# When the rows of one batch are scattered: as a burst at the start of the next batch, or spread over its first cross attention

## The chip, the cores and the metric

The kernel runs on one NeuronCore of a Trainium2 chip, as one launch. The metric is the device time of a run in microseconds. A core has five engines with queues of their own: TensorE (PE: matmuls and transposes), VectorE (DVE), ScalarE (ACT), GpSimd (POOL) and SyncE (SP, which here issues most of the DMAs). They wait for one another only through semaphores.

## The reference

A decoder of two layers on `x` of 4 batches x 512 tokens x 256 features, each sublayer behind a layer norm and with a residual:

```python
x = x + _L0_attn_ref(_layernorm(x), ...)    # A: 16 heads of 64, scores refined by a small MLP over heads
x = x + _L0_xattn_ref(_layernorm(x), ctx_1024, ctx_1024, ...)  # B: 16 heads of 16, 1024 keys
x = x + _L0_ffn_ref(_layernorm(x), ...)     # C: switch-head attention
x = x + _L1_attn_ref(_layernorm(x), ...)    # D: causal, rope
x = x + _L1_xattn_ref(_layernorm(x), ctx_1024, ctx_1024, mask, ...)  # E: masked cross attention
x = x + _L1_ffn_ref(_layernorm(x), ...)     # F and G: a mixture of 32 experts, 8 of them for each token
```

In the last line each token's normalized row goes through the 8 experts that a gate picks, weighted, and through two shared experts.

## The kernel before

**Rounds and stages.** The four batches are four rounds. A round has six stages, A to F, one for each line above (F: the gate and the shared experts). Each of the five engines has its own program, written in the same order of stages: a hardware loop over the rounds (`Fori`) with the six stages in its body. SP runs its loop three times and has the fourth round written out. After each stage all five meet at a barrier (`Steps.end`: a drain, a semaphore increment, a wait for all five), and `end_round` is the last of these in a round. After the four rounds stage G does the chosen experts for all batches at once.

**Scattering.** Stage F computes, for each token, the 8 places in a DRAM tensor `slot_rows` (one region per expert) where its row must go (`slot8`), and completes the row in SBUF, `xn`: 256 normalized features, the token's number, 32 expert weights, 290 float32 in all. `to_slots` (L1356) then scatters `xn` to `slot_rows` in 32 indirect DMAs issued by POOL: 4 tiles of 128 tokens x 8 places, 128 rows of 1160 B each (L1360). In POOL's program it stands behind `end_round` (L2223 and on), so its 32 DMAs are issued while the other engines are in stage A of the next round, or, for the last batch, in the start of stage G. Each adds 16 to the semaphore `scattered`, which only SP waits for, late in stage G.

**`xn` and the layer norms.** `ln_dve` (L389) does the layer norm between two stages: statistics, one power on POOL (`ln_pool`, L406), then four scaled tiles into `xn`; `ln_pe` (L430) transposes `xn` for the next stage. Stage A doesn't write `xn` itself (its input comes from `f_xnA`, made in stage F of the round before), but the layer norm between A and B does.

**The head of stage A.** PE projects q and k (L1757), multiplies them to scores (L1781) head by head and projects values (L1768) in between; DVE turns q and k by rope (L1956 to L1962); ACT copies each block of scores out of PSUM into `a_fin` (L1916); SP stores them to DRAM in another layout (L1710) and loads them back. The head ends when PE starts the small MLP (L1798). PE's next scores wait for ACT's copy (`s_up`), ACT waits for PE's scores (`s_mm`), DVE for the projections (`qk_mm`).

**Stage B.** After projections and 12 x 6 moves of q and k parts to their places (L455, issued by SP), an inner loop runs over 16 heads in pairs: PE scores (L532) for DVE's row maxima (L771), turned scores (L588) for ACT's exponentials (L709, 128 of them, semaphore `exp`), then the weighted sum (L605). DVE splits each head's maxima in three bfloat16 parts by small operations (L739 to L742). `OT`, a buffer of attn16_mem in SBUF, takes the finished heads' sums (L717); nothing uses it before the inner loop.

Of the kernel before, what the change touches and what calls it, by code (L numbers as in the profile page):

```python
# [22 lines left out]
P = 128  # L23
B, S, DM = 4, 512, 256
NI = S // P
# [5 lines left out]
STAGES = "ABCDEF"  # L31
# [161 lines left out]
TOPK = 8  # L193
# [26 lines left out]
def y_tile(ps, stage, i):  # L220

    if stage == "C":
        return ps[:, 2 + i, 0:Y_COLS]
    return ps[:, 7 - i // 2, (i % 2) * Y_COLS:(i % 2 + 1) * Y_COLS]
# [5 lines left out]
def decoder(nc, io, out, rounds=B):  # L230
    ctx = ExitStack()
    with ctx:
        def sb(name, shape, dt=F32):
            return ctx.enter_context(nc.sbuf_tensor(name, shape, dt))

        def sem(name):
            s = ctx.enter_context(nc.semaphore(name))
            counting.append(s)
            return s
# [4 lines left out]
        x = sb("x", [P, NI, DM])  # L244
        xn = sb("xn", [P, NI, ROW])
        xnT = sb("xnT", [P, KD, S])
        ctxT = sb("ctxT", [P, KD, CTX])
        ident = sb("ident", [P, P])
# [27 lines left out]
        slot8 = sb("slot8", [P, NI, TOPK], U32)  # L276
# [15 lines left out]
        ps = ctx.enter_context(nc.psum_tensor("ps", [P, 8, BANK], F32))  # L292
# [10 lines left out]
        scattered = ctx.enter_context(nc.semaphore("scattered"))  # L303
# [3 lines left out]
        ln_pow = sem("ln_pow")  # L307
        ln_xn = sem("ln_xn")
# [11 lines left out]
        sm = {}  # L320
# [8 lines left out]
        def scope(fn):  # L329
            with ExitStack() as inner:  # L330
                return fn(lambda name, shape, dt=F32: inner.enter_context(nc.sbuf_tensor(name, shape, dt)))
# [22 lines left out]
            return m  # L354

        M16 = scope(attn16_mem)

        WIDTH = {"B": 2560, "D": 3584, "E": 2560, "C": 3616}
        ORDER = [s for s in "BCDE" if s in STAGES]
# [6 lines left out]
        def ln_stats(ch, rows, var, early=()):  # L366
            for i in set(range(NI)) - set(early):
                last = nc.vector.bn_stats(out=st6[:, i, :], in_=rows(i))
            ch.link(last)
            for i in range(NI):  # L370
                last = nc.vector.bn_aggr(out=mv[:, i, :], in_=st6[:, i, :])
            ch.link(last)
            nc.vector.tensor_scalar(mv[:, :, 1], mv[:, :, 1], 1e-5, None, ALU.add).then_inc(var, 1)  # L373

        def ln_scaled(dve, ch, rows, powered, n, done, to=xn):
            dve.wait_ge(powered, n + 1)

            ch.link(nc.vector.tensor_tensor(rt[:, :], rstd[:, :], rstd[:, :], ALU.mult))
            ch.link(nc.vector.scalar_tensor_tensor(out=rt[:, :], in0=rt[:, :], scalar=-0.5, in1=mv[:, :, 1], op0=ALU.mult, op1=ALU.mult))
            ch.link(nc.vector.scalar_tensor_tensor(out=rstd[:, :], in0=rt[:, :], scalar=1.5, in1=rstd[:, :], op0=ALU.add, op1=ALU.mult))  # L380
            for i in range(NI):
                nc.vector.tensor_scalar(to[:, i, 0:DM], rows(i), mv[:, i, 0:1], rstd[:, i:i + 1],
                                        ALU.subtract, ALU.mult).then_inc(done, 1)
# [5 lines left out]
        def ln_dve(dve, ch, n, before):  # L389
            if before == "A":  # L390
                ln_stats(ch, lambda i: x[:, i, :], ln_var, EARLY[before])
                ln_scaled(dve, ch, lambda i: x[:, i, :], ln_pow, n, ln_xn)
                return
            rows = lambda i: y_tile(ps, before, i)
            ln_stats(ch, rows, ln_var, EARLY[before])
            ln_scaled(dve, ch, rows, ln_pow, n, ln_xn)
            if before == "C":
                last = nc.vector.tensor_copy(x[:, :, :], ps[:, 2:2 + NI, 0:Y_COLS])
            else:
                for h in range(2):  # L400
                    last = nc.vector.tensor_copy(x[:, 2 * h:2 * h + 2, :], ps[:, 7 - h, :].rearrange("p (i c) -> p i c", i=2))
            last.then_inc(x_kept, 1)

        def ln_pool(pool, n):
            pool.wait_ge(ln_var, n + 1)
            nc.gpsimd.tensor_tensor(rstd[:, :], mv[:, :, 1], half[:, :], ALU.pow).then_inc(ln_pow, 1)  # L406
# [21 lines left out]
                nc.tensor.matmul(ps[:, bank, :], identb[:, :], mneg[:, 0, 0:BANK], start=True, stop=True)  # L428

        def ln_pe(pe, n):  # L430
            for i in range(NI):
                pe.wait_ge(ln_xn, NI * n + i + 1)
                for k in range(KD):
                    last = nc.tensor.transpose(ps[:, k, i * P:(i + 1) * P], xn[:, i, k * P:(k + 1) * P], ident[:, :])
            last.then_inc(ln_tr, 1)

        def ln_act(act, n):
# [6 lines left out]
        def a16_sp(sp, c):  # L444
            m = M16
            g = lambda n: sm[c.name, n]
            sp.dma_start(m["KS"][KR:KST, :, :].rearrange("p h n -> p (h n)").bitcast(mybir.dt.uint16), io["k_unit"].partition_broadcast(3)).then_inc(g("k_ones"), 16)
            for kind, t, gr in c.moves:
                n = S if kind == "q" else c.nk
                stack, parts, order = (m["QS"], m["QP"], QPART) if kind == "q" else (m["KS"], m["KP"], KPART)  # L450
                last = max(k for k, e in enumerate(c.split_order) if c.tiles[e][:2] == (kind, t))
                sp.wait_ge(g("split"), last + 1)
                first, width = HEAD_GROUPS[gr]
                for r, a in enumerate(order):
                    sp.dma_start(stack[HD * r:HD * (r + 1), 8 * t + first:8 * t + first + width, 0:n],  # L455
                                 parts[HD * first:HD * (first + width), a, t, 0:n]).then_inc(g(f"stack_in{3 * t + gr}"), 16)

        def a16_pool(pool, ch, c):
            vp = M16["VP"][:, 0:c.nj, :, :].rearrange("p j h d -> p (j h) d")
            ch.link(nc.gpsimd.memset(vp[:, :, HD:32], 0.0))  # L460
            nc.gpsimd.memset(vp[:, :, HD:HD + 1], 1.0).then_inc(sm[c.name, "v_zero"], 1)

        def a16_pe(pe, c, n):
            m = M16
            g = lambda s: sm[c.name, s]
# [193 lines left out]
        def a16_act(act, c, n):  # L659
            m = M16  # L660
            g = lambda s: sm[c.name, s]
# [70 lines left out]
        def a16_dve(dve, ch, c):  # L732
            m = M16
            g = lambda s: sm[c.name, s]
# [159 lines left out]
        C_BACK = {s + 1: q for s, q in C_WEIGH.items()}  # L894

        def c_pe(pe, _, n, st):
            m = MC
            g = lambda s: sm["C", s]
# [289 lines left out]
        slot_rows = nc.dram_tensor("slot_rows", (NE * ROOM + P, ROW), F32, kind="Internal").ap()  # L1188
# [164 lines left out]
        EXTRA["F"] = dict(pe=f_pe, act=f_act, dve=f_dve, pool=lambda pool, *_: next_pool(pool), sp=f_sp)  # L1353


        def to_slots(pool):  # L1356

            for i in range(NI):
                for k in range(TOPK):
                    nc.gpsimd.indirect_dma_start(out=slot_rows, out_offset=bass.IndirectOffsetOnAxis(ap=slot8[:, i, k:k + 1], axis=0),  # L1360
                                                 in_=xn[:, i, :], in_offset=None).then_inc(scattered, 16)

        RX, RT, RH, RY = 9, 3, 3, 24
        NT = B * NI
# [73 lines left out]

        def g_pool(pool):
            g = lambda s: sm["G", s]  # L1440
            pool.wait_ge(x_stored, 16)
            pool.wait_ge(zeroed, 16 * NACC)
            for b in range(NBLOCK):
                pool.wait_ge(g("y_up"), b + 1)
                if b >= NACC:
                    pool.wait_ge(g(f"added{b % NACC}"), 16 * (b // NACC))
                nc.gpsimd.indirect_dma_start(out=sums[b % NACC], out_offset=bass.IndirectOffsetOnAxis(ap=token[:, b % RY:b % RY + 1], axis=0),  # L1447
                                             in_=MG["y"][:, b % RY, :], in_offset=None, compute_op=ALU.add).then_inc(g(f"added{b % NACC}"), 16)
# [767 lines left out]
        @block.gpsimd  # L2216
        def _(pool):
            st = Steps(pool, bars, False)
            setup_pool(pool)
            st.end()  # L2220
            st.end_round()
            with pool.Fori(0, rounds) as b:
                ch = Chain(pool, pool_chain)  # L2223
                for n, s in enumerate(STAGES):
                    if n:
                        ln_pool(pool, n - 1)
                    if s in CFG:
                        a16_pool(pool, ch, CFG[s])
                    else:
                        EXTRA[s]["pool"](pool, ch, n, st)  # L2230
                    st.end()
                st.end_round()
                to_slots(pool)
            g_pool(pool)

        @block.scalar
# [172 lines left out]
```

## Time and profile before

| | |
|---|---|
| median of 3 runs | 3875.18 us (3869.48 to 3879.73) |
| the profiled execution's own time | 3884.64 us |
| its span, first to last instruction | 3882.9 us |
| PE busy | 3455.5 us (89%) |
| DVE busy | 2416.0 us (62%) |
| ACT busy | 1803.9 us (46%) |
| POOL busy | 512.9 us (13%) |
| POOL, the 128 scattering DMAs, L1360 | 127.5 us, 996 ns each |

How to read it: the span holds a short setup, four rounds of some 850 to 875 us, and stage G of some 380 us. A busy share is a mean over stages; what a change in one stage is worth is read in that stage. The time of an indirect DMA on POOL is that of its issue, not of its transfer.

### The profile page before, as it was taken

The numbers are of one execution on the slowest core, as the hardware profiler recorded it, in microseconds if no ns is written. First come the engines' busy times: TensorE is split into PE (matmuls) and PEld (weight loads), VectorE is DVE, ScalarE is ACT, GpSimd is POOL, SyncE is SP. The second block draws the span as 40 slices with busy tenths as digits, with TensorE's granted clock in tenths as the row PEclk, the third lists the DMA queues.
The fourth block names the chain that finished last, engine by engine and source line by source line (L and its number), as shares of the span: only waits on it lengthen the run. The fifth ranks groups of instructions, "written<-read, shape, count | busy, mean of one in ns | idle before, by whom it ended". The sixth has DMA issues, their size and how long they took to land.

```text
span 3882.9 us, 62857 instructions
## 1 busy us (share of the span) xinstructions
PE 3455.5 (89%) x21953; PEld 1668.0 (43%) x21953; DVE 2416.0 (62%) x6385; ACT 1803.9 (46%) x3597; POOL 512.9 (13%) x451
## 2 busy tenths in 40 slices
PE   6999989997999889996999889997999889997992
PEld 2352445343362445342352445343352445344772
DVE  5668576854668576853668576853668576853553
ACT  2755434442755434442755434442745434442441
POOL 0000020003000020003000020003000020006885
PEclk9999999998999999998999999998999999997996
DMA  6313001215313001214313001215313201847998
GB/s 211 115 39 64 20 6 48 46 58 157 109 40 63 20 8 46 46 58 150 115 39 64 20 7 47 45 58 167 107 35 61 90 9 46 234 160 172 160 161 172
DMA packets 184288, 317.59 MB, mean 82 GB/s; under 512 B 29972, under 2 KB 139412, under 8 KB 178580
## 3 DMA queue, kind: packets, MB, share of 16 engines
q1 hardware_dynamic: 152888, 270.90, 25.1%
q0 software_dynamic: 29040, 39.86, 5.8%
q8 instruction: 187, 3.06, 0.3%
q10 hardware_dynamic: 2032, 2.61, 0.2%
q14 instruction: 141, 1.16, 0.1%
HBM read 176.94 MB, written 116.70 MB: 76 GB/s over the span
## 4 chain that ended last, share of the span: by engine, by line
PE 68%; DVE 19%; ACT 4%; issue 3%; another core or an unknown queue 3%; DMA 1%; PEldq 1%; SPq 1%; POOL 0%; DVEq 0%; PEld 0%; POOLq 0%; ACTq 0%
PE ps L605 8%; PE ps L588 6%; PE ps L428 5%; PE ps L532 4%; DVE mx L771 4%; PE ps L1860 4%; PE ps L1467 3%; PE ps L593 3%; PE ps L1798 3%; PE ps L484 2%; PE ps L1781 2%; DVE ps L768 2%; PE ps L1757 2%; PE ps L1482 2%
## 5 line engine op out<-in xcount | busy, mean ns | idle before, releaser
L709 ACT ACTIVATE PT<-ps 128x512 f32<-128x512 f32 (+2 forms) x1280 | 643.8, 564 | 332.8 <-PE ps L593 174.6
L771 DVE TENSOR_REDUCE mx<-ps 128x1 f32<-128x512 f32 (+3 forms) x768 | 431.0, 617 | 91.6 <-PE ps L532 49.1
L588 PE MATMUL ps<-QS,KS 99*128 99x512 bf16 (+2 forms) x1280 | 421.1, 370 | 8.5 <-ACT PT L709 8.0
L532 PE MATMUL ps<-KS,QS 96*128 96x512 bf16 (+3 forms) x1280 | 397.1, 373 | 17.5 <-DVE mx L771 7.3
L406 POOL TENSOR_TENSOR rstd<-mv,half 128x4 f32<-128x4 f32 x20 | 20.3, 1016 | 2829.8 <-DVE mv L373 2829.8
L768 DVE CUSTOM_DVE_ANT_0 ps<-ps,mneg 128x512 f32<-128x512 f32 x512 | 340.7, 718 | 82.2 <-PE ps L532 79.0
L605 PE MATMUL ps<-PT,VP 128*32 128x512 f32 (+3 forms) x2560 | 377.1, 577 | 0.0
L428 PE MATMUL ps<-mneg,identb 128*128 128x512 bf16 x1240 | 330.6, 395 | 29.3 <-DVE a_fin L1975 10.9
L588 PEld LDWEIGHTS ps<-QS,KS 99*128 99x128 bf16 x1280 | 108.6, 97 | 395.5 <-ACT PT L709 234.5
L1447 POOL DMA_INDIRECT sums<-wbuf,ctxT x159 | 247.9, 1559 | 57.4 <-issue 37.2
L1975 DVE TENSOR_TENSOR a_fin<-a_fin,ps 128x512 f32<-128x512 f32 (+1 forms) x176 | 104.5, 635 | 210.2 <-PE ps L1840 208.7
L532 PEld LDWEIGHTS ps<-KS,QS 96*128 96x128 bf16 x1280 | 128.4, 100 | 226.0 <-DVE mx L771 74.2
L698 ACT ACTIVATE QS<-ps 3x512 bf16<-3x512 f32 x192 | 113.3, 590 | 234.1 <-PE ps L570 231.7
L1940 ACT ACTIVATE a_X<-ps,b1A 128x1024 f32<-128x1024 f32 (+2 forms) x152 | 169.3, 1157 | 73.4 <-PE ps L1804 72.8
L593 PE MATMUL ps<-mnegT,identb 128*128 128x512 bf16 x512 | 194.6, 380 | 0.0
L428 PEld LDWEIGHTS ps<-mneg,identb 128*128 128x128 bf16 x1240 | 119.0, 101 | 167.1 <-issue 32.0
L1916 ACT ACTIVATE a_fin<-ps 128x2048 f32<-128x2048 f32 (+1 forms) x64 | 79.2, 1237 | 214.8 <-PE ps L1781 116.4
L1467 PE MATMUL ps<-g_W,g_xT 128*128 x636 | 167.3, 386 | 4.9 <-issue 4.9
L1757 PE MATMUL ps<-wbuf,a_Y 128*128 128x512 f32 x256 | 134.0, 668 | 22.3 <-issue 12.1
L791 DVE RECIPROCAL rq<-ps 128x16 f32<-128x16 f32 x48 | 12.4, 258 | 224.7 <-PE ps L542 224.7
L1928 ACT ACTIVATE a_fin<-a_fin,a_nm 128x512 f32<-128x512 f32 (+3 forms) x256 | 140.5, 550 | 2.2 <-DVE a_nm L1985 1.6
L1360 POOL DMA_INDIRECT slot_rows<-xn,slot x128 | 127.5, 996 | 78.1 <-remote 40.3
(332 smaller groups left out, 6020.7 us busy)
## 6 DMA issues: line engine op xcount, KB each, us to landing
slot_rows<-in_padrows SPq DMA_DIRECT2D x32, 725.0 KB, 19.8
scores<-a_fin SPq DMA_DIRECT2D x64, 256.0 KB
a_fin<-scores SPq DMA_DIRECT2D x32, 512.0 KB, 4.6
KS<-KP SPq DMA_DIRECT2D x240, 64.0 KB, 2.6
g_xb<-slot_rows SPq DMA_DIRECT2D x105, 145.0 KB
a_Y<-in_wA SPq DMA_DIRECT2D x4, 3072.0 KB, 13.6
scores<-a_fin SPq DMA_DIRECT2D x64, 192.0 KB
a_fin<-scores SPq DMA_DIRECT2D x12, 1024.0 KB, 7.9
```

The lines of the kernel that those rows point to most:

```text
L428: nc.tensor.matmul(ps[:, bank, :], identb[:, :], mneg[:, 0, 0:BANK], start=True, stop=True)
L532: last = nc.tensor.matmul(o, m["QS"][0:KR, h, i * P:(i + 1) * P], m["KS"][0:KR, h, f:f + w], start=True, stop=not c.causal)
L588: last = nc.tensor.matmul(o, m["KS"][0:KST, h, j * P:(j + 1) * P], m["QS"][0:KST, h, q0:S], start=True, stop=plain)
L593: last = nc.tensor.matmul(o, identb[:, :], mnegT[:, j, :], start=False, stop=True)
L605: last = nc.tensor.matmul(ps[r:r + 32, 6, q0:S], m["VP"][:, j, h, :], m["PT"][:, mp % 2, j % 2, e, 0:S - q0], start=(j == 0), stop=(j == c ...
L709: nc.scalar.activation(m["PT"][:, mp % 2, j % 2, e, 0:w], ps[:, SLOTS + n % TURNED, 0:w], ACT.Exp, scale=HD ** -0.5).then_inc(g("exp"), 1)
L768: nc.vector.tensor_tensor_reduce(ps[:, k % SLOTS, 0:w], ps[:, k % SLOTS, 0:w], mneg[:, i, f:f + w], 1.0, NEG, ALU.add, ALU.max, m["mx"][:, ...
L771: nc.vector.tensor_reduce(m["mx"][:, h % 2, i, f // BANK:f // BANK + 1], ps[:, k % SLOTS, 0:w], AX.X, ALU.max, negate=True).then_inc(g("sl ...
L1447: nc.gpsimd.indirect_dma_start(out=sums[b % NACC], out_offset=bass.IndirectOffsetOnAxis(ap=token[:, b % RY:b % RY + 1], axis=0), in_=MG["y ...
L1467: last = nc.tensor.matmul(ps[:, 2 + b % 2, 0:2 * P], m["xT"][:, b % RT, k, :], m["W"][:, bass.ds(e, 1), 2 * P * k:2 * P * (k + 1)].rearran ...
L1757: last = nc.tensor.matmul(ps[:, 4 + e % 4, :], m["w"][:, k, col:col + P], xnTA[:, k, :], start=(k == 0), stop=(k == KD - 1))
L1940: nc.scalar.activation(m["hid"][k % 2][:, n * x:n * x + n, 0:w], ps[:, A_UP + n * x:A_UP + n * x + n, 0:w], ACT.Gelu, bias=b1A[:, 0:1]).th ...
```

## The change

The scatter of a batch's rows is taken out of the place behind `end_round`. POOL's program has the first round written out (`one_round(True)`), then a loop of three rounds with a stage B in which POOL waits for the 24th exponential, issues one scattering DMA, waits for three more exponentials, issues the next, and so on to the 117th of 128. The last batch's 32 stay a burst, at the start of `g_pool`. So that `xn` stays whole until then, the layer norm between A and B writes its rows into `xnB`, a view of half of the buffer `OT`, and `ln_pe` reads them there.

```diff
         M16 = scope(attn16_mem)
+        xnB = M16["OT"][:, 0:2, :].rearrange("p e (i c) -> p (e i) c", c=DM)
...
             if before == "A":
                 ln_stats(ch, lambda i: x[:, i, :], ln_var, EARLY[before])
-                ln_scaled(dve, ch, lambda i: x[:, i, :], ln_pow, n, ln_xn)
+                ln_scaled(dve, ch, lambda i: x[:, i, :], ln_pow, n, ln_xn, xnB)
                 return
...
         def ln_pe(pe, n):
+            rows = xnB if STAGES[n] == "A" else xn
...
-        def to_slots(pool):
-
-            for i in range(NI):
-                for k in range(TOPK):
-                    nc.gpsimd.indirect_dma_start(out=slot_rows, out_offset=bass.IndirectOffsetOnAxis(ap=slot8[:, i, k:k + 1], axis=0),
-                                                 in_=xn[:, i, :], in_offset=None).then_inc(scattered, 16)
+        EXP_FIRST, EXP_STEP = 24, 3
+
+        def to_slot(k):
+
+            i, k = divmod(k, TOPK)
+            nc.gpsimd.indirect_dma_start(out=slot_rows, out_offset=bass.IndirectOffsetOnAxis(ap=slot8[:, i, k:k + 1], axis=0),
+                                         in_=xn[:, i, :], in_offset=None).then_inc(scattered, 16)
...
         def g_pool(pool):
             g = lambda s: sm["G", s]
+            for k in range(NI * TOPK):
+                to_slot(k)
             pool.wait_ge(x_stored, 16)
...
-            with pool.Fori(0, rounds) as b:
+            def one_round(first):
                 ch = Chain(pool, pool_chain)
                 for n, s in enumerate(STAGES):
                     if n:
                         ln_pool(pool, n - 1)
                     if s in CFG:
                         a16_pool(pool, ch, CFG[s])
+                        if s == "B" and not first:
+                            for k in range(NI * TOPK):
+                                pool.wait_ge(sm["B", "exp"], EXP_FIRST + EXP_STEP * k)
+                                to_slot(k)
                     else:
                         EXTRA[s]["pool"](pool, ch, n, st)
                     st.end()
                 st.end_round()
-                to_slots(pool)
+
+            one_round(True)
+            with pool.Fori(0, rounds - 1) as b:
+                one_round(False)
             g_pool(pool)
```

POOL's program before, from the layer norm ahead of stage E to the end of the loop's body (L406 and L413 are the norms' powers, L460 and L461 fill `VP` at the start of a cross attention, L1360 is the scatter, L2222 closes the loop):

```order
L406 TENSOR_TENSOR rstd<-mv,half 128x4
L460 MEMSET VP 128x128x16
L461 MEMSET VP 128x128
L406 TENSOR_TENSOR rstd<-mv,half 128x4
L413 TENSOR_TENSOR rstd<-mv,half 128x4
L1360 DMA slot_rows<-xn,slot 69760x290 x32
L2222 REGISTER_ALU
L2222 COMPARE_AND_BRANCH
```

And POOL's program of the change, from the end of the written-out first round into stage C of the loop's body (L414 is the last norm's power, L407 that ahead of stage B, L1363 the scatter, L1077 the first work of stage C):

```order
L407 TENSOR_TENSOR rstd<-mv,half 128x4
L414 TENSOR_TENSOR rstd<-mv,half 128x4
L2244 UNCONDITIONAL_BRANCH
L407 TENSOR_TENSOR rstd<-mv,half 128x4
L462 MEMSET VP 128x128x16
L463 MEMSET VP 128x128
L1363 DMA slot_rows<-xn,slot 69760x290 x32
L407 TENSOR_TENSOR rstd<-mv,half 128x4
L1077 TENSOR_TENSOR c_tmp<-c_at,c_msk 128x512
```

The 32 DMAs stood behind the last norm of a round, with nothing between them; they now stand behind the `VP` fill of stage B and ahead of the power for the norm between B and C, each behind a wait for `exp`.

DVE's norm between A and B before (`ln_scaled`, with the first work of B behind it), and below it that of the change:

```order
L378 TENSOR_TENSOR rt<-rstd 128x4
L379 SCALAR_TENSOR_TENSOR rt<-rt,mv 128x4
L380 SCALAR_TENSOR_TENSOR rstd<-rt,rstd 128x4
L382 TENSOR_SCALAR xn<-x,mv,rstd 128x256 x4
L740 TENSOR_TENSOR rest<-val,KP 128x512
```

```order
L379 TENSOR_TENSOR rt<-rstd 128x4
L380 SCALAR_TENSOR_TENSOR rt<-rt,mv 128x4
L381 SCALAR_TENSOR_TENSOR rstd<-rt,rstd 128x4
L383 TENSOR_SCALAR OT<-x,mv,rstd 128x256 x4
L742 TENSOR_TENSOR rest<-val,KP 128x512
```

Only the target of the four scaled tiles is another, `OT` in the place of `xn`; the order is the same. PE, ACT and SP have the same instructions in the same order as before.

## Rows read from the trace of the kernel before

**Rows 1.** Busy time by stretch: the head of stage A in the four rounds.

```profile
core 0: us, PE busy (x) PEld busy (x) DVE busy (x) ACT busy (x) POOL busy (x), PEclk, DMA share, GB/s
37.05:108.78 71.73, 71.39 (x366) 30.09 (x366) 30.54 (x49) 27.13 (x26) 0.00 (x0) 1.00 0.56 173
890.53:979.50 88.97, 74.95 (x367) 31.57 (x367) 30.55 (x49) 26.58 (x26) 29.90 (x30) 0.89 0.62 192
1761.54:1856.64 95.10, 72.75 (x366) 30.65 (x366) 30.64 (x49) 25.87 (x25) 28.24 (x29) 0.87 0.57 180
2634.21:2723.40 89.19, 74.43 (x367) 31.48 (x367) 30.56 (x49) 26.19 (x26) 29.44 (x30) 0.89 0.61 190
```

**Rows 2.** Busy time by stretch: the rest of stage A in two rounds.

```profile
109.00:277.70 168.70, 157.40 (x1826) 81.84 (x1814) 112.16 (x339) 110.84 (x191) 0.00 (x0) 0.99 0.20 67
...
1856.60:2025.20 168.60, 157.34 (x1827) 82.16 (x1827) 112.17 (x339) 110.83 (x191) 0.01 (x1) 0.99 0.19 66
```

**Rows 3.** Timeline of POOL: start, length, instruction, idle before it and its releaser.

```profile
887.06 1.20 POOL L1360 DMA_INDIRECT slot_rows<-xn,slot  x1 [9.93 <-remote]
...
928.31 0.96 POOL L1360 DMA_INDIRECT slot_rows<-xn,slot  x1 [0.30 <-issue]
...
1797.36 0.96 POOL L1360 DMA_INDIRECT slot_rows<-xn,slot  x1 [0.30 <-issue]
```

**Rows 4.** Timeline of ACT in the heads of rounds 2, 3 and 4.

```profile
911.76 1.88 ACT L1916 ACTIVATE a_fin<-ps 128x2048 f32<-128x2048 f32 x1 [20.51 <-remote]
...
931.88 1.02 ACT L1916 ACTIVATE a_fin<-ps 128x1024 f32<-128x1024 f32 x1 [10.80 <-remote]
...
1802.08 1.88 ACT L1916 ACTIVATE a_fin<-ps 128x2048 f32<-128x2048 f32 x1 [40.98 <-remote]
...
2675.50 1.02 ACT L1916 ACTIVATE a_fin<-ps 128x1024 f32<-128x1024 f32 x1 [12.12 <-remote]
```

**Rows 5.** Timeline of PE, head of round 3: the scores behind ACT's first copy.

```profile
1804.01 2.94 PE L1781 MATMUL ps<-a_X 32*128 32x384 f32 x16 [22.10 <-ACT a_fin L1916]
```

**Rows 6.** Waits of the whole kernel: total us, times, longest us.

```profile
ACT a_fin L1916 <- remote: 97.7, 6, 41.0
...
DVE a_X L1956 <- remote: 22.3, 3, 11.3
```

**Rows 7.** DMA queues from 1757 to 1802 us: packets, MB, share of 16 engines.

```profile
q0 software_dynamic: 1536, 4.75, 28.5%
...
q14 instruction: 6, 0.05, 0.4%
q8 instruction: 2, 0.03, 0.4%
```

**Rows 8.** Busy time by stretch: most of the inner loop of stage B, round 1.

```profile
343.00:428.00 85.00, 79.39 (x470) 24.96 (x469) 60.38 (x136) 62.42 (x118) 0.00 (x0) 1.00 0.00 1
```

**Rows 9.** DMA issues from 274 to 443 us: KB, us from issue to landing.

```profile
wbuf<-in_wC SPq DMA_DIRECT2D x1, 1808.0 KB, 8.3
```

**Rows 10.** Timeline of SP, ACT and DVE in stage B of round 1.

```profile
334.05 0.59 SPq L2177 DMA_DIRECT2D wbuf<-in_wC  x1
...
340.26 1.08 ACT L709 ACTIVATE PT<-ps 128x512 f32<-128x512 f32 x2
...
421.41 2.06 ACT L709 ACTIVATE PT<-ps 128x512 f32<-128x512 f32 x4 [1.28 <-PE ps L588]
...
441.55 0.76 DVE L368 BATCH_NORM_STATS2 st<-ps 128x6 f32<-128x256 f32 x2 [0.27 <-DVEq L86]
```

**Rows 11.** Timeline of DVE at the start of stage G, beside the last batch's burst.

```profile
3506.41 0.17 DVE L1557 COPY ctxT<-ctxT 128x2 f32<-128x2 f32 x1
...
3507.45 0.26 DVE L1557 COPY ctxT<-ctxT 128x16 f32<-128x16 f32 x1
...
3509.84 0.40 DVE L1567 TENSOR_SCALAR table<-ctxT 128x2 int32<-128x2 f32 x1
```

**Rows 12.** Groups of POOL's instructions, whole kernel: busy us, mean ns, idle before.

```profile
L1447 POOL DMA_INDIRECT sums<-wbuf,ctxT x159 | 247.9, 1559 | 57.4 <-issue 37.2 <-DVE wbuf L1584 18.6 <-DMA sums<-wbuf,ctxT 1.5
```

**Rows 13.** Waits of PE from 3560 to 3860 us, in stage G.

```profile
PE ps L1482 <- ACT g_hT L1520: 0.9, 2, 0.5
```

More of the change, by code:

```diff
@@ L433, in ln_pe @@
                 for k in range(KD):
-                    last = nc.tensor.transpose(ps[:, k, i * P:(i + 1) * P], xn[:, i, k * P:(k + 1) * P], ident[:, :])
+                    last = nc.tensor.transpose(ps[:, k, i * P:(i + 1) * P], rows[:, i, k * P:(k + 1) * P], ident[:, :])
             last.then_inc(ln_tr, 1)
```

## The prediction

> **What bounds the kernel now.** I read the busy time by stretch first, cut at the same two instructions in every round: PE's first projection (L1757) and its first MLP matmul (L1798). The reader is to see one line that differs: the head of stage A takes 71.73 us in round 1 and 88.97, 95.10 and 89.19 us in rounds 2 to 4, with the same number of PE, DVE and ACT instructions (to within one record), and PE's busy time within 4 us [rows 1]. POOL's column is 0 in round 1 and about 29 us in the others: that is the scatter. The rest of stage A is the same with and without a burst ahead of it, 168.70 and 168.60 us [rows 2], so nothing that the head loses is made up later.
>
> Then the timelines of the heads. POOL issues a scatter every 0.96 + 0.30 = 1.26 us without a gap, from 887.06 us to 929.3 us in round 2 and to 1798.3 us in round 3 [rows 3]. ACT's copies of scores stand still until that is over: the last late one runs at 931.88 us, after 10.80 us of idleness, in round 3 the very first at 1802.08 us, after 40.98 us, in round 4 one at 2675.50 us [rows 4]. PE waits for ACT: its second block of scores starts at 1804.01 us, after 22.10 us of waiting for L1916 [rows 5]. In the waits of the whole kernel ACT's L1916 stands with 97.7 us and DVE's rope with 22.3 us, all put down to "remote", that is to a releaser that the profile doesn't name [rows 6]. (These totals hold time in which nothing could have run anyway, so I don't use them as a price; the stretches are the price.) I can't name the mechanism from this. It isn't the bandwidth of the DMA engines: the scatters take 28.5% of them in round 3's stall [rows 7].
>
> **What the change takes away.** The 32 scatters of three bursts (rounds 2, 3, 4) leave stage A's head. Its price is the head's excess over round 1, which does the same work without a burst: 88.97 - 71.73 = 17.24 us, 95.10 - 71.73 = 23.37 us, 89.19 - 71.73 = 17.46 us, together 58.07 us [rows 1]. The fourth burst, of the last batch, keeps its place ahead of stage G's own work: 0 us.
>
> What is late next in the head? Round 1's head is bound by PE, 71.39 of 71.73 us busy at a clock of 1.00 [rows 1], and its SP queue carries the same stores and the load of B's weights. Rounds 2 to 4 have one transfer more, the store of `x`, issued as the round begins, like POOL's first scatter at 887.06 us, and more than 20 us before ACT's first copy, 911.76 us, gives SP scores to store [rows 3, 4]; I cost it at 0.
>
> **What it adds in stage B.** 96 scatters beside three inner loops (rounds 2, 3, 4). Step by step:
>
> - The place is empty. SP issues C's weights at 334.05 us and they land 8.3 us later [rows 9, 10]; the 24th exponential, which opens the first scatter, is the second of the pair at 340.26 us [rows 10]. From 343 to 428 us the DMA engines are at 0.00 [rows 8]. So the scatters collide with about 1 us of one load that nobody needs before stage C.
> - The pace. The 117th exponential is the first of the four at 421.41 us [rows 10]. From the 24th to the 117th there are 31 gaps in (422.0 - 341.3) = 80.7 us, 2.60 us each, against 1.26 us of issue: POOL and the queue are about half loaded, where the burst loaded them fully.
> - The end. The last scatter is issued by about 423.3 us; the barrier at the end of B is at about 441.5 us, where DVE's first instruction of stage C waited for it [rows 10]. POOL arrives some 18 us early, even if its drain waits for the last transfers. Behind the waiting scatters on POOL stands only the norm's power ahead of stage C, which comes after that barrier. 0 us.
> - `xnB` for `xn`: the same four DVE instructions and eight transposes with another address: 0 us. Stage B itself writes `OT` only in its inner loop, long after them.
> - POOL's 32 waits and the written-out round: in stages A and B POOL has nothing else but the fill of `VP`, which stands ahead of them. 0 us.
>
> **The doubtful part: does an issue on POOL slow the inner loop?** DVE is 60.38 of 85.00 us busy there, PE 79.39 [rows 8], so both are near the bound and a slower handshake would count. Two rows bound it. In stage G POOL issues 159 indirect DMAs of 1.56 us [rows 12], more densely than the new ones, and PE waited 0.9 us in 300 us [rows 13]. From there the price is 0. In the last burst some of DVE's tiny operations are longer: copies of 2 columns take 0.17 us, one of 16 columns 0.26, a conversion of 2 columns 0.40 [rows 11]. Stage B has two small casts for each head and four copies, some 28 in the scattered stretch; at the worst lengthening, 0.40 - 0.17 = 0.23 us, that is 3 x 28 x 0.23 = 19 us. I take 1 us for all three rounds: most such operations in that burst have their usual length, POOL issues only half of the time, and stage G is the nearer row in kind.
>
> The rule that speaks against this change is in the Trainium skill, SBUF — State Buffer, section "Who interferes with whom": GpSimd and a DVE copy or cast in a mode that uses the second port pair exclude each other, and the one that came second waits for the whole of the other's instruction. By that rule a cast could wait 0.96 us, and the sum would be 3 x 28 x 0.96 = 81 us worse, which turns the gain into a loss. The trace doesn't bear it out at that size: the longest excess is 0.23 us.
>
> **Sum.** -58.07 + 1 = -57 us. In the profiled execution's own time 3884.64 - 57 = 3827.6 us; that execution is 9.5 us above the median of the three runs. From the median: 3875.18 - 57 = 3818 us. If the 9.5 us were all stall of the heads that unprofiled runs don't have, the gain would be 48.6 - 1 and the time 3827.6 us; the three runs spread over 10 us. The likeliest case's own range is therefore 3810 to 3828 us.
>
> **Rivals.**
>
> - *The stall forms again, smaller.* Near the end of B's inner loop four exponentials take 2.06 us [rows 10], so three come in 1.55 us, close to the burst's 1.26 us. Against it: that holds for some 8 scatters in 17 us, and in round 2 ACT's first copy after 24.7 us of burst still came at 911.76 us while the long waits came later [rows 4]. If each of three loops had half of the last wait of round 2, 5.4 us, the time is 3818 + 16 = 3834 us. 12%.
> - *The wait isn't the burst's.* Rounds 2 to 4 differ from round 1 in a second thing: every engine has just jumped back to the start of its loop, and its next instructions must be fetched. Then the 58 us stay and the time is 3875 us. For it: the releaser is unnamed. Against it: the waits end within 4 us of the burst's end, 929.3 and 931.88, 1798.3 and 1802.08 [rows 3, 4], and the instruction queues moved 8 packets, 0.09 MB, in those 45 us [rows 7]. The Trainium skill, Runtime: NRT & Kernel Launch, section "Instruction fetch mechanics", says that a taken branch forces a fetch before execution goes on; that would be such a stall, and no row here shows one of 20 us. 5%.
> - *Slower: POOL's issue holds up the inner loop.* If an instruction on the path in B waited for each issue in full, 96 x 0.96 = 92 us are added and the time is 3875 - 58 + 92 = 3909 us. It decides from 58.07 / 96 = 0.60 us for each scatter on. For it: DVE's maxima and PE take turns on the path, with little slack. Against: rows 11 to 13 as above. 5%.
>
> **How the numbers follow.** Likeliest case 78%, 3818 us. With the first rival's 12% the range reaches to 3836 us; downwards 3808 us, for runs whose stalls were larger than the profiled one's. The two other cases, 10%, are left out. A change of 0.3%, 12 us, is about what a measurement of this kernel can tell from none. Faster by more: 78 + 12 = 90, with the part of the slower rival that stays under 0.3 us a scatter 91%; same 5%; slower 4%.
>
> **What would show it.** Right: heads of stage A of about 72 us in all four rounds, no "remote" wait of ACT's L1916, PE's clock there near 1.00; POOL's scatters in rounds 2 to 4 spread over some 81 us of stage B; a stage B, from norm to norm, as long in round 2 as in round 1. Wrong: heads of 89 us without a scatter in them (the second rival), or a stage B that is longer by more than 5 us where it scatters than where it doesn't, with longer DVE rows (the third) or an unnamed wait of ACT or DVE near its end (the first).

## The result, and the profile after

The changed kernel takes 3820.59 us (median of 4 runs, 3819.91 to 3824.86) against 3876.36 us of the kernel before (4 runs), a ratio of 0.9858 [0.9846, 0.987]. Forecast were 3818.0 us and a range of 3808 to 3836. The profiled execution took 3820.71 us, with a span of 3819.0.

One plain fact has to stand ahead of all that follows: the experiments ran on three chips, and the kernel before takes about 3877 us on one of them, as in the comparison above, and 3809 and 3807 us on the other two. So the gain is one of the chip as much as of the kernel. Each chip was measured at one time only, so a property of the chip can't be told from one of that time; "chip" below stands for both. Each experiment is compared with the kernel before on its own chip.

The heads of stage A after, the four rounds by stretch (columns as in [rows 1]):

```profile
36.99:108.32 71.33, 70.99 (x366) 29.93 (x367) 30.56 (x49) 27.12 (x26) 0.00 (x0) 1.00 0.57 176
890.13:961.57 71.44, 71.09 (x366) 29.96 (x367) 30.56 (x49) 25.86 (x25) 0.00 (x0) 0.96 0.57 177
1739.32:1811.12 71.80, 71.46 (x367) 30.10 (x367) 30.56 (x49) 25.86 (x25) 0.00 (x0) 0.96 0.57 175
2589.47:2661.16 71.69, 71.35 (x367) 30.07 (x367) 30.56 (x49) 25.86 (x25) 0.00 (x0) 0.96 0.55 170
```

Rounds 2 to 4 now take what round 1 takes: (88.97 + 95.10 + 89.19) - (71.44 + 71.80 + 71.69) = 58.3 us are gone [rows 1]. ACT's first copy in round 3, which had stood 40.98 us [rows 4], comes after PE's scores:

```profile
1758.26 1.88 ACT L1921 ACTIVATE a_fin<-ps 128x2048 f32<-128x2048 f32 x1 [19.29 <-PE ps L1786]
1761.83 1.45 ACT L1921 ACTIVATE a_fin<-ps 128x1536 f32<-128x1536 f32 x1 [1.69 <-PE ps L1786]
```

In the waits of the whole kernel "remote" has lost ACT's copies and DVE's rope (97.7 and 22.3 us in [rows 6]). All that is left of it stands at the start of stage G:

```profile
POOL slot_rows L1363 <- remote: 11.3, 1, 11.3
DVE ctxT L1546 <- remote: 5.2, 1, 5.2
ACT g_hT L1525 <- remote: 2.4, 1, 2.4
DVE ctxT L1588 <- remote: 0.6, 1, 0.6
```

The scatters stand in stage B, one behind another at 1.5 to 4.6 us from start to start, from 1191.05 to 1271.80 us in round 2 (timeline of POOL):

```profile
1191.05 1.20 POOL L1363 DMA_INDIRECT slot_rows<-xn,slot  x1 [57.59 <-ACT PT L711]
1193.24 0.98 POOL L1363 DMA_INDIRECT slot_rows<-xn,slot  x1 [1.00 <-ACT PT L711]
...
1271.80 0.96 POOL L1363 DMA_INDIRECT slot_rows<-xn,slot  x1 [1.90 <-ACT PT L711]
```

And stage B by stretch, from one norm's power on POOL to the next, rounds 1 to 4. Round 1 has no scatters in it:

```profile
276.80:442.16 165.36, 155.31 (x784) 57.42 (x783) 115.17 (x255) 91.36 (x170) 3.11 (x3) 0.97 0.22 42
1130.29:1292.60 162.31, 151.34 (x784) 56.90 (x783) 115.25 (x255) 91.36 (x170) 34.76 (x36) 1.00 0.31 72
1979.90:2143.44 163.54, 152.60 (x784) 57.07 (x783) 115.26 (x255) 91.36 (x170) 34.60 (x35) 0.99 0.31 72
2829.91:2995.40 165.49, 155.38 (x784) 57.47 (x783) 115.26 (x255) 91.36 (x170) 34.61 (x36) 0.97 0.30 71
```

POOL issues 31 us of DMAs in the three later ones, and their length doesn't tell them from the first. What does differ, 162 or 165 us, goes with PE's column and its granted clock (1.00 or 0.97).

### The profile page after: what moved, and what is told of

Same layout as the page of the kernel before. It is cut to its first block, busy times and chain, and to the rows that moved or that the text cites. A ratio compares the mean times of both kernels' runs of the same rounds, so it can differ in the third digit from the quotient of the medians.

```text
span 3819.0 us, 62855 instructions
## 1 busy us (share of the span) xinstructions
PE 3441.5 (90%) x21953; PEld 1664.1 (44%) x21953; DVE 2416.8 (63%) x6385; ACT 1804.2 (47%) x3597; POOL 511.0 (13%) x451
## 4 chain that ended last, share of the span: by engine, by line
PE 70%; DVE 19%; ACT 4%; issue 3%; SPq 1%; DMA 1%; PEldq 1%; another core or an unknown queue 1%; POOL 0%; PEld 0%; POOLq 0%; DVEq 0%; ACTq 0%
PE ps L607 8%; PE ps L590 7%; PE ps L429 5%; DVE mx L773 5%; PE ps L534 4%; PE ps L1865 4%; PE ps L1472 4%; PE ps L1762 3%; PE ps L595 3%; PE ps L1803 3%; PE ps L486 2%; PE ps L1786 2%; DVE ps L770 2%; PE ps L1487 2%; PE ps L638 2%
## 5 line engine op out<-in xcount | busy, mean ns | idle before, releaser
L607 PE MATMUL ps<-PT,VP 128*32 128x512 f32 (+3 forms) x2560 | 375.4, 576 | 0.0
L407 POOL TENSOR_TENSOR rstd<-mv,half 128x4 f32<-128x4 f32 x20 | 20.3, 1015 | 2499.1 <-DVE mv L374 2499.1
L1363 POOL DMA_INDIRECT slot_rows<-xn,slot x128 | 126.0, 984 | 348.5 <-ACT PT L711 327.7
```

What stands on the lines that cost most here:

```text
L607: last = nc.tensor.matmul(ps[r:r + 32, 6, q0:S], m["VP"][:, j, h, :], m["PT"][:, mp % 2, j % 2, e, 0:S - q0], start=(j == 0), stop=(j == c ...
```

## The experiments

The prediction left open whose signal was late. The trace settles it: beside the instructions it records when each semaphore rises. The scores' semaphore `s_mm` rises once for each of the 16 blocks of a head. In round 1 of the kernel before each rise stands 0.04 or 0.05 us behind the end of PE's block. In round 3 the first block ends at 1779.99 us and the semaphore rises at 1802.05 us, 22.06 us later; ACT's first copy starts at 1802.08 us [rows 4]. PE wasn't held up by that block, for it began its next projections at once:

```profile
1777.99 2.00 PE L1781 MATMUL ps<-a_X 32*128 32x512 f32 x16
1779.92 1.98 PE L1757 MATMUL ps<-wbuf,a_Y 128*128 128x512 f32 x4
```

In round 2 the first three rises are 2.45, 2.97 and 9.58 us late, in round 4 they are 1.14, 5.71 and 9.96 us late, and all others of both heads 0.04 or 0.05 us. The rises that DVE and ACT cause in these heads are never more than 0.01 us late. So PE's signals are what is late in the kernel before, and they are late only under the burst, the last of them until 4 us behind its end. In the changed kernel's head of round 2 all 16 rises are again 0.04 or 0.05 us behind their blocks.

What it takes to make them late is the subject of the runs. Two theories were put to the test. **Train**: an unbroken train of scatters holds back signals between engines wherever it stands. **Place**: only the head of stage A suffers from it.

### First chip, on which the kernel before takes 3809.22 us (3798.58 to 3817.19, 26 runs)

**A full burst of spare scatters at the start of stage A**, added to the changed kernel in rounds 2 to 4 (the same rows and places, into a spare tensor, 1160 B each):

```diff
+                    if s == "A" and not first:
+                        for k in range(32):
+                            nc.gpsimd.indirect_dma_start(out=spare_rows, out_offset=bass.IndirectOffsetOnAxis(ap=slot8[:, k // TOPK, k % TOPK:k % TOPK + 1], axis=0),
+                                                         in_=xn[:, k // TOPK, 0:290], in_offset=None).then_inc(spared, 16)
```

> The changed kernel, with 32 more scatters of the same 1160 B rows to a spare DRAM tensor, as a burst at the start of stage A in rounds 2 to 4 (the real ones stay spread in stage B). If the burst alone makes the heads slow, whoever else jumps or loads there: three heads of 89 to 95 us, +58 us, about 3879 us. If the old heads were slow for another reason that the change removed by the way (the order of POOL's barrier, the layout of its loop), the heads stay near 72 us and the time near 3821 us.

Measured: 3811.54 us, ratio 1.0000 [0.9988, 1.0012]. Its round 2 by stretch, and ACT's first copy in it:

```profile
887.35:958.96 71.61, 71.28 (x366) 30.16 (x366) 30.62 (x49) 25.85 (x25) 29.38 (x30) 0.96 0.76 239
```

```profile
906.11 1.88 ACT L1924 ACTIVATE a_fin<-ps 128x2048 f32<-128x2048 f32 x1 [18.90 <-PE ps L1789]
```

The burst is there (29.38 us of POOL), and the head doesn't notice it: PE's signals are at most 0.05 us late in it. A head near 72 us had been expected only for the case that the old heads were slow for some other reason than the burst. But on this chip the kernel before takes 3809 us itself, so there was no stall to bring back, and the run can't decide that.

**The burst in stage B**: all 32 real scatters from the 24th exponential on.

```diff
-                                pool.wait_ge(sm["B", "exp"], EXP_FIRST + EXP_STEP * k)
+                                pool.wait_ge(sm["B", "exp"], EXP_FIRST)
```

> The changed kernel with all 32 scatters issued at the 24th exponential of stage B, without waits between them. Theory 'train': an unbroken train of about 40 us on POOL holds back the signals between engines wherever it stands, so stage B loses 15 to 25 us in each of rounds 2 to 4, unnamed waits appear, and the time is about 3865 to 3890 us. Theory 'place': only the head of stage A, with its stores of scores and its load, is hurt; B has no other transfer, and the time stays near 3821 us.

Measured: 3810.91 us, ratio 1.0002 [0.9992, 1.0011]; stages B of 162.16, 165.54, 163.55 and 163.66 us.

**The burst in stage A behind its head**: the real scatters, once the small MLP has begun, none in stage B.

```diff
+                        pool.wait_ge(sm["A", "w1"], 1)
+                        for k in range(NI * TOPK):
+                            to_slot(k)
```

> The changed kernel with the 32 scatters as an unbroken burst in stage A, but behind the head, from the first block of the MLP on. Theory 'train': 15 us or more are lost in each of three rounds, 3865 us or more. Theory 'place': near 3821 us, since only a few loads of scores run there.

Measured: 3810.57 us, ratio 1.0002 [0.9991, 1.0012].

**The scatters paced in the head**: two behind each of its 16 blocks of scores, none in stage B.

```diff
+                        for k in range(NI * TOPK):
+                            pool.wait_ge(sm["A", "s_mm"], k // 2 + 1)
+                            to_slot(k)
```

> The changed kernel with the scatters back in the head of stage A of the next round, two of them after each of the 16 blocks of scores (a block about every 3.3 us). Theory 'train': with gaps the signals come through, heads of 72 to 76 us, 3821 to 3833 us. Theory 'place': the scatters collide with the stores of scores in whatever order, heads of 85 us or more, above 3860 us.

Measured: 3838.01 us, ratio 1.0065 [1.0044, 1.0086], 29 us slower than the kernel before, whose burst stands in the same head. Its round 2 by stretch, ACT's wait, and the stores of scores from 886 to 967 us (median us to landing, where the view gives one):

```profile
886.93:967.03 80.10, 71.45 (x366) 30.11 (x367) 30.56 (x49) 25.54 (x25) 32.55 (x32) 0.95 0.71 210
```

```profile
ACT a_fin L1921 <- DMA scores<-a_fin: 12.5, 9, 2.8
```

```profile
scores<-a_fin SPq DMA_DIRECT2D x16, 192.0 KB, 5.2
scores<-a_fin SPq DMA_DIRECT2D x16, 128.0 KB, 4.0
```

In the run with the burst behind the head, on the same chip, the same stores of round 2 landed in 2.9 and 2.6 us. This is an ordinary collision. The head stores its scores all the time, and the stores land later beside the scatters; ACT waits for them before it writes `a_fin` again, and PE, at the head's end, waits for the scores to be loaded back, which it doesn't do in the changed kernel:

```profile
PE ps L1803 <- DMA a_fin<-scores: 19.9, 3, 7.2
```

That is most of what the three heads lose against round 1: 80.10 + 78.52 + 79.06 - 3 x 71.73 = 22.5 us. It has nothing to do with the unnamed waits: PE's signals are at most 0.10 us late in round 2's head.

On this chip all placements but one cost the same, so train and place could not be told apart there. What it told is that the burst alone doesn't make the wait.

### Second chip, before 3877.15 us (3872.9 to 3885.42, 13 runs)

**Both kernels again, as they are.**

> The kernel before, unchanged, for its profile beside the others. In the last comparison its median was 3809 us, where the profiled one that the prediction rests on took 3885 us, and a burst in the head of stage A cost nothing. If the stall belongs to a chip and not to the kernel, this run shows either heads of 72 us and about 3809 us, or heads of 89 to 95 us and about 3876 us, one of the two throughout, in the profile and in all times. If it is a matter of chance in each execution, the two mix within one chip.

> The changed kernel, unchanged. Where before has heads of 72 us, the change has nothing to take away: same time as before, 3807 to 3813 us, ratio 1.000. Where before has heads of 89 us or more: 3820 us, ratio 0.986.

Measured: 3881.26 us, ratio 1.0006 [0.9995, 1.0016], and 3816.59 us, ratio 0.9834 [0.9817, 0.9852]. Heads of rounds 2 to 4 of the kernel before, by stretch:

```profile
885.52:975.40 89.88, 73.06 (x366) 30.76 (x367) 30.68 (x49) 26.20 (x26) 27.96 (x29) 0.87 0.60 190
1752.84:1848.48 95.64, 73.12 (x366) 30.79 (x367) 30.70 (x49) 25.85 (x25) 28.18 (x29) 0.85 0.56 178
2626.79:2718.57 91.78, 75.56 (x365) 31.92 (x367) 30.69 (x49) 25.85 (x25) 27.91 (x29) 0.86 0.58 184
```

The stall is that of [rows 1] again, to within 2.6 us a head.

**The burst in stage B again**: the kernel that was worth 1.0002 on the first chip.

> The scatters as an unbroken burst in stage B from the 24th exponential on. Where before stalls in its heads, theory 'train' expects 15 to 25 us lost in each of three loops of B (about 3870 us), theory 'place' none (3821 us). Where before doesn't stall: the same as before, 3809 to 3812 us.

Measured: 3927.74 us (3924.14 to 3934.47), ratio 1.0121 [1.0104, 1.0138]. Its stages B by stretch, rounds 1 and 2:

```profile
277.35:442.64 165.29, 154.68 (x781) 57.40 (x783) 115.06 (x255) 91.32 (x170) 3.11 (x3) 0.97 0.22 42
1130.60:1329.74 199.14, 159.51 (x781) 57.96 (x783) 115.64 (x255) 91.75 (x170) 34.07 (x35) 0.89 0.25 59
```

With 200.54 and 203.91 us in rounds 3 and 4 the three make 603.59 us. In the changed kernel on this chip they took 163.72, 165.42 and 163.42, together 492.56. That is 111.0 us, and the medians differ by 3927.74 - 3816.59 = 111.2 us. For this chip train is right and place is wrong. The waits of this kernel, and then PE, ACT and DVE in the burst of round 2, which begins at 1194.50 us:

```profile
ACT PT L711 <- remote: 119.8, 40, 23.4
DVE mx L773 <- remote: 83.6, 8, 25.0
```

```profile
1210.45 0.61 PE L590 MATMUL ps<-QS,KS 99*128 99x512 bf16 x1
1220.23 0.61 PE L590 MATMUL ps<-QS,KS 99*128 99x512 bf16 x1 [9.17 <-ACT PT L711]
1220.63 0.63 PE L534 MATMUL ps<-KS,QS 96*128 96x512 bf16 x1
1225.29 0.61 PE L534 MATMUL ps<-KS,QS 96*128 96x512 bf16 x1 [4.03 <-DVE mx L773]
```

```profile
1204.69 1.23 ACT L711 ACTIVATE PT<-ps 128x512 f32<-128x512 f32 x2 [0.33 <-PE ps L590]
1219.58 0.60 ACT L711 ACTIVATE PT<-ps 128x512 f32<-128x512 f32 x1 [13.66 <-remote]
```

```profile
1224.54 0.69 DVE L773 TENSOR_REDUCE mx<-ps 128x1 f32<-128x512 f32 x1 [14.66 <-remote]
```

Of the first line 32 waits, 49.1 us, aren't the burst's: they stand in stage E, and the kernel before and the changed kernel have them too in their profiles on this chip ("49.1, 32, 2.5"). The other 8 stand in stage B and make 70.7 us.

The reader is to see the direction. PE's matmul of 1210.45 us is over by 1211.06, and PE issues no other until 1220.23; yet ACT, which waits for just such a matmul, goes on at 1219.58, 8.5 us later. The other way nothing is late: ACT is done at 1220.18 and PE starts at 1220.23; DVE is done at 1225.23 and PE starts at 1225.29. So the "remote" releaser is PE's own signal that its matmul is done.

The recorded rises of the semaphores bear it out. The last of the weighted sums that PE starts at 1204.68 us (L607) ends at 1205.74, and the semaphore that it raises, for which ACT waits too, rises at 1218.09, 12.35 us later, while PE goes on to start further matmuls from 1205.68 to 1210.45. That of the matmul L572, which ends at 1210.52, rises at 1237.08, 26.56 us later. The rises that ACT and DVE cause stand 0.01 us behind their instructions all through the burst.

The first long lateness stands some 11 us behind the start of the burst (ACT's idleness begins at 1205.92); before it PE's signals are up to 1.9 us late, from about 1203 us on, and ACT's waits are below 2.3 us. On the first chip the same burst leaves PE's signals at most 0.05 us late in rounds 2 and 3.

**Half a burst of spare scatters at the start of stage A**: the diff of the full one, with `range(16)`.

> The changed kernel with a burst of only 16 scatters to a spare tensor at the start of stage A. Where before stalls, 'it takes 20 us of unbroken train' expects nearly no loss (3821 to 3826 us), 'each scatter holds something up' half of the loss (about 3850 us). Where before doesn't stall: 3809 to 3812 us.

Measured: 3819.33 us, ratio 0.9848 [0.9831, 0.9865]; its round 2 by stretch:

```profile
884.77:957.20 72.43, 71.47 (x365) 30.11 (x367) 30.69 (x49) 25.85 (x25) 13.16 (x14) 0.96 0.66 204
```

Half of the scatters cost about 1 us of each head where all of them had cost 18.7 to 24.5 (above, less round 1's 71.18). That doesn't prove that short trains are harmless: ACT's first copy isn't due until the 16 are all issued, so few of PE's signals could be late. The trace has a projection's signal late even so in round 2, by 2.38 us, and a block of scores' in round 4, by 2.08 us.

### Third chip, before 3807.36 us (3800.95 to 3816.48, 31 runs)

**The changed kernel once more.**

> The changed kernel as it is, beside the next three. Where the kernel before takes about 3877 us, the change should again give a ratio of 0.983 to 0.987 (3812 to 3825 us). Where the kernel before takes about 3809 us, as it did beside the first four experiments, its heads of stage A have no excess to give back, and both theories expect a ratio of 0.999 to 1.001.

Measured: 3809.68 us, ratio 1.001 [1.0, 1.0019]. Here the change is worth nothing.

**The burst in stage B with a wait for landing after each 8** (POOL's three later rounds written out, so that the waits are on constants):

```diff
+                                if k % 8 == 7:
+                                    pool.wait_ge(scattered, 16 * (NI * TOPK * done + k + 1))
```

> The 32 scatters of rounds 2 to 4 stand in stage B as in the burst there, all from the 24th exponential on, but after each 8 of them POOL waits until all so far have landed. Theory of the backlog (late signals come from scatters that pile up in the queue): a wait for the landing empties it each time, no unnamed wait of over 3 us in stage B, a stage B of 162 to 168 us and 3815 to 3830 us where the kernel before takes about 3877. Theory of the rate (what counts is the share of time in which scatters are issued, and a pause of some 3 us in 13 changes little): a stage B of 185 to 200 us and 3880 to 3920 us. Where the kernel before takes about 3809 us, both expect no difference.

**A full burst of thin spare scatters at the start of stage A**, 128 B rows:

```diff
-                                                         in_=xn[:, k // TOPK, 0:290], in_offset=None).then_inc(spared, 16)
+                                                         in_=xn[:, k // TOPK, 0:32], in_offset=None).then_inc(spared, 16)
```

> The changed kernel with a burst of 32 further scatters at the start of stage A in rounds 2 to 4, of 128 rows of 128 B each to a spare tensor: as many descriptors as the burst before, a ninth of its bytes. If the number of descriptors is what delays the signals, the heads of stage A take 85 to 95 us and the kernel 3865 to 3880 us where the kernel before takes about 3877. If the bytes do it, the heads take 71 to 74 us and the kernel 3815 to 3825 us. Where the kernel before takes about 3809 us, both expect no difference.

Measured: 3808.36 us, ratio 0.9999 [0.9987, 1.0011], and 3807.2 us, ratio 0.9999 [0.9989, 1.0008]. Both could have spoken only on the second chip, and stay inconclusive.

**The last burst parted in two**:

```diff
             for k in range(NI * TOPK):
+                if k == NI * TOPK // 2:
+                    pool.wait_ge(g("xt_up"), 8)
                 to_slot(k)
```

> The changed kernel, its last burst (32 scatters at the start of stage G) parted in two: POOL issues the second 16 only when eight blocks of stage G have been turned and copied. Theory of the unbroken train: stage G, 414 to 416 us from the last norm's power to the end where the kernel before takes about 3877, loses the 16 us for which PE waited there and takes 404 to 409 us, and the kernel is 7 to 11 us faster than the changed one beside it. Rival (stage G ends with POOL's accumulating DMAs or DVE's work, so a hole at its start is made up later, or POOL's later start costs as much): within 3 us of the changed kernel. Where the kernel before takes about 3809 us, both expect no gain.

Measured: 3813.70 us (3810.2 to 3817.64), ratio 1.0014 [1.0004, 1.0024], so 4.0 us slower than the changed kernel beside it. Why it was tried: on the second chip the changed kernel has a hole in PE's timeline in stage G, under the burst that was left in place, and on the third chip the same kernel has none. Both by stretch, 21 us from 59 us after the last norm's power on:

```profile
3461.00:3482.00 21.00, 2.86 (x6) 1.88 (x7) 0.41 (x2) 1.60 (x5) 11.93 (x13) 0.50 0.34 115
```

```profile
3459.70:3480.70 21.00, 21.00 (x113) 16.58 (x112) 11.39 (x38) 10.33 (x38) 16.43 (x16) 1.00 0.76 200
```

And POOL's accumulating DMAs of stage G (duration, first and last start), in the changed kernel on the third chip and, as L1454, with the parted burst:

```profile
L1452 POOL DMA_INDIRECT sums<-wbuf,ctxT x159: 1555/1559/1612, 3475.9 to 3770.2; - x159
```

```profile
L1454 POOL DMA_INDIRECT sums<-wbuf,ctxT x159: 1555/1559/1611, 3484.0 to 3778.3; - x159
```

They stand behind the burst on POOL and take 294.3 us in either kernel. From the last norm's power they begin 3475.9 - 3400.67 = 75.2 us later in the one and 3484.0 - 3403.64 = 80.4 us in the other: of the pause of 6.30 us in the burst 5.1 us go into the end. So the ground of the rival on record with this run, that POOL's later start costs as much, is borne out, though 4.0 us is more than the 3 us it allowed. What the parting would give back on the second chip wasn't measured.

## Why the prediction was right, point by point

- **The heads' excess**, forecast -58.07 us, measured -58.3. That the burst was its cause is shown on the second chip: the same 32 DMAs put a stall of 35 to 40 us into each stage B when they stand there in a burst, and none at 2.6 us apart. (The prediction's "stand still until that is over" was too strong: in round 2 two blocks came through during the burst, 2.45 and 2.97 us late.)
- **What is late next**: PE, as forecast; 71.1 to 71.5 us busy in heads of 71.4 to 71.8. Its clock there is 0.96, not the "near 1.00" that was to show it: a slip of 0.04 that the length of the head doesn't show.
- **The pace in stage B**, forecast 80.7 us from the first scatter to the last: 1271.80 - 1191.05 = 80.75 us in round 2.
- **Stage B**, forecast +1 us for three rounds. The three later ones average 163.78 us, the first took 165.36, and rounds without scatters vary by as much; so +1 can't be told from 0. The better measure is DVE's busy time: 115.25 and 115.26 against 115.17 us, 0.3 us in three rounds. (DVE was called "near the bound" there; at 60.38 of 85.00 us it had 24 us to spare, and PE alone was near it.)
- **The sum.** The profiled execution was forecast at 3827.6 us and took 3820.71; the median at 3818 and took 3820.59. The span fell by 63.9 us, 58.3 of it in the heads. Of the rest, stages D hold 3.6 us (427.67 against 424.09) and stages B 2.6 us (659.26 against 656.70): the same steps of 2 and 3 us with PE's clock that round 1 shows too, no work of the change's.
- **The first rival**, the stall forms again, smaller: it didn't. POOL's shortest spacing in round 2 was 1.47 us, for single pairs. But its mechanism is real: with all at 1.26 us the stall is there in stage B, and larger than in stage A. The choice of the 24th and each third exponential therefore does work, on the chip that stalls.
- **The second rival**, the loop's jump: refuted. PE, ACT and DVE jump as before, and rounds 2 to 4 have heads of 71.4 to 71.8 us; and the stalls of stage B came with the burst alone, on the same jumps. Nor was ACT late to take its signal: it starts 0.03 us after the semaphore rises in round 3. The Trainium skill's rule on fetching after a taken branch (Runtime: NRT & Kernel Launch, "Instruction fetch mechanics") has no visible price in these heads. They begin with PE's first projection behind the jump, so what a jump costs ahead of it isn't in them.
- **The third rival**, POOL's issue holds up the inner loop: refuted at 0.3 us instead of 92. The Trainium skill's rule (SBUF — State Buffer, "Who interferes with whom") had given an estimate of 81 us; for the issue of indirect DMAs the trace shows no such wait: the nine casts (L741) that ran beside an issue took 0.19 us at most, and 0.18 is usual elsewhere. Whether these casts run in the mode that the rule names isn't shown by any run here, so this says how little the estimate applied and doesn't refute the rule.
- **What the prediction said it could not name** is half named: the late releaser is PE's signal, and it is late only under a train of scatters; what holds it back isn't known. What it left out altogether is the chip. It took the stall for a property of the kernel. On the other two chips the kernel before is already at 3809 and 3807 us, so there the heads have little or nothing to give back, and on the one of them where it ran the same change is worth 1.001. That the forecast of 3818 us came true is in this part luck: it needed a chip that stalls.
- The difference between the chips is found to within 4 us: 63.8 us in the heads of the repeated kernel before (89.88 + 95.64 + 91.78 - 3 x 71.18), and in stage G 416.23 against 406.63 us for the same changed kernel. Together 73 us, against 3877 - 3808 = 69 us between the medians of the kernel before; for the changed kernel stage G's 9.6 us stands against 3816.59 - 3809.68 = 6.9.

What stays open: why PE's signals were held back on one chip and not on two, on the same program with the same 1.26 us of spacing, and whether that is the chip's or the hour's; whether it is the number of rows or their bytes; and whether a short wait for landing is enough to stop it. The changed kernel stays the best that was measured on the second chip; no variant was faster than the kernel before, clear of noise, on the other two.

## What to carry to other kernels

Spread a burst of indirect DMAs over a stretch where the DMA engines are idle (56 us gained where the burst stalled, nothing where it didn't), not over one that stores all the time (29 us lost here). Before a stall is taken for the kernel's, run the kernel before again on another chip: the same instructions took 58 to 64 us longer in three heads on one. And when a wait is "remote", look which of the two directions between a pair of engines is late: here three rows told PE's signals from those of ACT and DVE. Behind a burst at a queue's end, ask what the same engine issues next: in stage G a pause in the burst moved 159 accumulating DMAs.

## What the runs showed of the hardware that wasn't expected

- On one of three chips PE's signals to ACT and DVE come late under 32 back-to-back scatters of 128 x 1160 B at 1.26 us each: by 22.06 us in a head of stage A and 26.56 us in a stage B, with waits of up to 25.0 us, while ACT's and DVE's signals are at most 0.01 us late in the same stretches. Elsewhere the same burst costs nothing: in stages A and B on the first chip, in G on the third.
- The lateness doesn't begin with the burst: in stage B PE's signals were 1.9 us late some 8 us into it, and the first long wait began after 11 us.
- 96 indirect DMAs issued beside an inner loop in which PE is busy for 79.39 and DVE for 60.38 of 85.00 us lengthened DVE's busy time by 0.3 us in all.
- Stages with the same instructions differ by 2 or 3 us with PE's granted clock (stage B: 162.31 us at 1.00, 165.36 at 0.97), which sets how small a term a single profile can show.
